# Routed rows written straight into their slots while the shared experts run, in place of one-hot lists and gathers

## Time and profile before

| what | us |
|---|---|
| median of 3 runs | 513.04 |
| lowest, highest | 508.51, 518.37 |
| the profiled execution, whole | 506.99 |
| the profiled execution, span | 505.3 |
| granted clock of TensorE, mean | 0.999 of full speed |

### The profile page before, as it was taken

One profiled execution on the slowest core, in us unless ns is written; L12 is line 12 of the kernel. 1 busy time (PEld: TensorE's weight loads), 2 busy tenths in 40 slices (PEclk: granted clock), 3 DMA queues, 4 the chain that ended last, 5 costly groups with the idle time before them and its releaser, 6 DMA issues.

```text
span 505.3 us, 10018 instructions
## 1 busy us (share of the span) xinstructions
PE 490.5 (97%) x3071; PEld 448.2 (89%) x3072; DVE 355.4 (70%) x765; ACT 261.1 (52%) x525; POOL 249.9 (49%) x367
## 2 busy tenths in 40 slices
PE   8999999999999999989999999999999899999996
PEld 7998988888888889988889999999998899888886
DVE  3666778898987556766676677676675666479896
ACT  3567785556663445565455555545554444444322
POOL 2042246655551454666967767677667674211100
PEclk9999999999999999999999999999999999999999
DMA  8387569156222234534344444444444442599942
GB/s 225 130 281 224 169 186 310 57 179 201 45 83 43 84 93 126 119 103 125 104 114 116 114 116 123 123 117 117 112 114 116 115 105 68 145 370 322 384 140 83
DMA packets 104938, 74.54 MB, mean 148 GB/s; under 512 B 61946, under 2 KB 99844, under 8 KB 104900
## 3 DMA queue, kind: packets, MB, share of 16 engines
q1 hardware_dynamic: 95780, 55.21, 37.1%
q0 software_dynamic: 6816, 18.62, 12.5%
q10 hardware_dynamic: 2304, 0.26, 0.5%
HBM read 40.25 MB, written 20.32 MB: 120 GB/s over the span
## 4 chain that ended last, share of the span: by engine, by line
PE 75%; DVE 15%; ACT 5%; issue 4%; DMA 1%; another core or an unknown queue 0%; DVEq 0%; ACTq 0%
PE bank L274 17%; PE bank L276 17%; PE bank L275 17%; PE bank L790 9%; PE bank L762 5%; PE bank L792 5%; DVE bank L1222 2%; ACT gt_h L952 1%; DVE acc L1333 1%; DVE xt_l L1034 1%; ACT x_half L872 1%; DVE x L1058 1%; DVE pos L1081 1%; DMA xin<-in_x_dram 1%; PE bank L576 1%
## 5 line engine op out<-in xcount | busy, mean ns | idle before, releaser
L274 PE MATMUL bank<-w_all,rt_h 128*128 x284 | 97.6, 344 | 0.0
L276 PE MATMUL bank<-w_all,rt_l 128*128 x284 | 91.6, 323 | 0.0
L275 PE MATMUL bank<-w_all,rt_h 128*128 x284 | 91.5, 322 | 0.0
L790 PE MATMUL bank<-w_all,gt_h 128*128 (+1 forms) x213 | 78.0, 396 | 0.2 <-issue 0.2
L551 POOL DMA_INDIRECT y_rows<-y_sb,dst_i x71 | 72.5, 1021 | 11.2 <-POOL spare L465 10.4
L544 POOL DMA_INDIRECT rows<-x_halves,tok_i x71 | 69.5, 978 | 12.5 <-issue 2.2
L952 ACT CAST gt_h<-bank 128x512 fp32r<-128x512 f32 (+1 forms) x48 | 28.1, 586 | 88.7 <-DVE bank L1222 79.8
L274 PE MATMUL bank<-xs_h,sg_h 128*128 128x512 f32 x176 | 70.6, 401 | 0.3 <-DVE gt_h L1233 0.3
L275 PE MATMUL bank<-xs_l,sg_h 128*128 128x512 f32 x176 | 68.9, 391 | 0.0
L276 PE MATMUL bank<-xs_h,sg_l 128*128 128x512 f32 x176 | 68.7, 390 | 0.0
L1295 DVE TENSOR_TENSOR g<-bank,act 128x352 f32<-128x352 f32 x71 | 37.2, 524 | 41.7 <-issue 24.5
(11 more groups left out here) (180 smaller groups left out, 1155.6 us busy)
## 6 DMA issues: line engine op xcount, KB each, us to landing
pick<-y_rows SPq DMA_DIRECT2D x16, 512.0 KB, 7.8
xin<-in_x_dram SPq DMA_DIRECT2D x8, 512.0 KB, 4.8
x_halves<-x_half SPq DMA_DIRECT2D x8, 512.0 KB, 3.3
w_own<-in_L_ffn_w_gate_dram SPq DMA_DIRECT2D x8, 352.0 KB, 4.5
w_own<-in_L_ffn_w_up_dram SPq DMA_DIRECT2D x8, 352.0 KB, 4.7
y_sb<-in_x_dram SPq DMA_DIRECT2D x5, 512.0 KB, 3.5
base_rows<-y_sb SPq DMA_DIRECT2D x5, 512.0 KB, 2.8
acc<-base_rows SPq DMA_DIRECT2D x5, 512.0 KB, 7.1
```

Source lines behind the costliest of these rows:

```text
L274: pe.matmul(o, lh, rh, start=start, stop=False, skip_group_check=skip)
L275: pe.matmul(o, lh, rl, start=False, stop=False, skip_group_check=skip)
L276: return pe.matmul(o, ll, rh, start=False, stop=stop, skip_group_check=skip)
L790: pe.matmul(YE[par][:, 0:2 * D].rearrange("p (h d) -> p h d", h=2), gt_h[par][0:n, cols], both, start=(c == 0), stop=False, skip_group_che ...
```

## The change

No list of rows by slot is made. While the shared experts run, SP loads each 128-row tile of `x1_halves` into SBUF, twice side by side (`load_stage`, 4 buffers), POOL puts the number of the output row behind each row (`number`), and two indirect DMAs of 128 rows write the tile to its slots in a new DRAM tensor `slot_rows` of 9088 rows of 1056 bytes (`put`, 64 of them, with 7 more for the empty slots). The routed stage then turns the rows of a block straight from `slot_rows` (`turn_rows`, four buffers), and reads all output row numbers back in one DMA (9088 elements of 4 bytes) into `dst_i`. POOL does no gathers.

Low halves of experts 2 to 7 and of groups 2 to 4 move from POOL to DVE (`weights_low`, `rows_low`). DVE's one-hots and `list_out`, and PE's 64 `permute` matmuls go. `rank` moves one unit on. The weights of the two choices (7 small DVE steps) move to unit 25. In the routed stage `r_high(1)`/`e_silu(0)` and `r_low(1)`/`e_mul(0)` change places. At the very end the last low half is made in two pieces, and one of the last three stores is issued by ACT. The core of the diff (buffers and semaphores left out):

```diff
@@ SP
+        STORE_AT = (6, 9, 18, 28)
+            def load_stage(t):
+                b = t % N_STAGE
+                sp.wait_ge(s_put[b], 16 * (pads_in(b) + TOPK * (t // N_STAGE)))
+                sp.dma_start(stage[b][:, :, 0:2 * D], x1_dram[t * P:(t + 1) * P, :].rearrange("(o p) d -> p o d", o=1)
+                             .broadcast_to([P, TOPK, 2 * D])).then_inc(s_stage[b], 16)
             def turn_rows(i):
-                sp.wait_ge(s_row[i % 3], 16 * (i // 3 + 1))
-                if i >= 2:
-                    sp.wait_ge(s_rlo, i - 1)
-                    sp.wait_ge(s_rhi, i - 1)
-                sp.dma_start_transpose(turned[i % 2][:], rows[i % 3][:]).then_inc(s_turn[i % 2], 16)
+                if i >= 4:
+                    sp.wait_ge(s_rlo, i - 3)
+                    sp.wait_ge(s_rhi, i - 3)
+                sp.dma_start_transpose(turned[i % 4][:], slot_dram[i * P:(i + 1) * P, 0:2 * D]).then_inc(s_turn[i % 4], 16)
...
             load_expert(5)
+            store_base(0)
+            load_res(1)
+            for t in range(4):
+                load_stage(t)
             sp.wait_ge(s_blk, 1)
             load_expert(7)
             load_expert(6)
-            for j in range(NPG - 1):
-                store_base(j)
-                load_res(j + 1)
-                if j + 3 <= NPG:
-                    load_raw(j + 3, raw)
+            for t in range(4, NT):
+                if t in STORE_AT:
+                    j = STORE_AT.index(t)
+                    if j >= 1:
+                        store_base(j)
+                        load_res(j + 1)
+                    if j + 3 <= NPG:
+                        load_raw(j + 3, raw)
+                load_stage(t)
+            for b in range(N_STAGE):
+                sp.wait_ge(s_put[b], 16 * (pads_in(b) + TOPK * (NT // N_STAGE)))
+            sp.wait_ge(s_top_w, 1)
             for i in range(4):
                 turn_rows(i)
+            sp.dma_start(dst_i[:].bitcast(U16).rearrange("p (b h) -> p b h", h=2),
+                         slot_dram[:, 2 * D:2 * D + 2].rearrange("(b p) h -> p b h", p=P)).then_inc(s_dst, 16)
+            for i in range(4, 6):
+                turn_rows(i)
             store_base(NPG - 1)
-            for i in range(4, NBLK):
+            for i in range(6, NBLK):
                 turn_rows(i)
@@ POOL
+            def number(b):
+                return stage[b][:, :, 2 * D:2 * D + 2].bitcast(I32)
+            def put(b, c, where):
+                pool.indirect_dma_start(slot_dram, bass.IndirectOffsetOnAxis(ap=where, axis=0),
+                                        stage[b][:, c, :], None).then_inc(s_put[b], 16)
             pool.wait_ge(s_x1, NT)
...
+            for i in range(2):
+                pool.wait_ge(s_x1st[i], 16 * (NG // 2))
+            for b in range(N_STAGE):
+                ins = pool.memset(stage[b][:], 0)
+            link(ins)
+            for n in range(PADS):
+                b, c = n % N_STAGE, n // N_STAGE
+                link(pool.tensor_copy(number(b)[:, c, :], pad_ids[:, n:n + 1]))
             split_low(1)
             pool.wait_ge(s_mark, 1)
...
             routed_low(1)
-            routed_low(2)
...
-            routed_low(6)
+            pool.wait_ge(s_pad_i, 1)
+            for n in range(PADS):
+                put(n % N_STAGE, n // N_STAGE, pad_i[:, n:n + 1])
+            pool.wait_ge(s_slot_i, 1)
+            for t in range(NT):
+                b = t % N_STAGE
+                pool.wait_ge(s_stage[b], 16 * (t // N_STAGE + 1))
+                link(pool.tensor_copy(number(b), ids[:, :, t:t + 1]))
+                for c in range(TOPK):
+                    put(b, c, slot_i[:, c, t:t + 1])
...
-            for i in range(5):
-                gather(i)
+            pool.wait_ge(s_dst, 16)
             for i in range(NBLK):
-                if i + 5 < NBLK:
-                    gather(i + 5)
                 if i == 14:
                     split_low(NPG)
                 scatter(i)
@@ PE
                 gate(j, c)
+                if u == RANK_AT + 1:
+                    rank()
                 if u >= 2:
                     down(*order[u - 2])
-                for t in hot_tiles(u - 2):
-                    permute(t)
                 up(j, c)
-                if u == RANK_AT:
-                    rank()
@@ DVE
+            def weights_low(e, i):
+                own_ap, hi, lo = routed_part(e, i)
+                v.wait_ge(s_whi, TURN_OF[e] * N_PART + i + 1)
+                v.tensor_tensor(lo, own_ap, hi.bitcast(F32), ALU.subtract).then_inc(s_wlo, 1)
...
-            steps_at = {0: (0, 8), 1: (3, 6), 2: (3, 6), 3: (3, 6), 4: (3, 1000), 5: (0, 6), 6: (0, 6), 7: (3, 7), 8: (3, 1000)}
+            steps_at = {0: (0, 8), 1: (3, 6), 2: (3, 6), 3: (1, 0)}
+            places_at = {4: (0, 4), 5: (3, 6), 6: (3, 6), 7: (3, 8), 8: (3, 1000)}
+            low_at = {10: (2, 0), 11: (2, 2), 13: (3, 0), 14: (3, 2), 16: (4, 0), 17: (4, 2), 19: (5, 0), 20: (5, 2),
+                      22: (7, 0), 23: (7, 2), 26: (6, 0), 27: (6, 2)}
...
+                if c in (2, 3) and j + 1 in BY_V:
+                    rows_low(j + 1, c - 2)
+                if u in low_at:
+                    e, i = low_at[u]
+                    weights_low(e, i)
+                    weights_low(e, i + 1)
+                if u == NPRE - 5:
+                    some(weigh, 1000)
```

228 lines of the change are left out of this document (96 added, 132 removed).

## The result

The changed kernel took 535.76 us (median of 4 runs, 535.27 to 539.57) beside 511.88 us (4 runs) for the kernel before on the same chip: ratio 1.053, 95% interval 1.044 to 1.061, slower. The forecast was 523.0 us, slower by 1.9%. Its direction and its place hold; the chain cost more than twice what was forecast. The profiled execution took 539.57 us, its span is 537.8 us.

A forecast was written before the change was run, and what follows sets the result against it. PE bounds the kernel, busy 490.5 of 505.3 us. Terms -4.2 + 13.3 + 2.0 + 0 - 0.5 - 0.6 = +10.0 us gave 523.0 us, 1.9% slower; the 8-in-10 range was 500 to 536 us.

The forecast's parts named there:

- +13.3: PE's stall in us before its first routed block, wanted at 181.3 us and ready at 194.6; bounds 7.1 and 20.2.
- (c): POOL's pitch per tile: number write 0.18, 0.17 until the put, two puts of 1.02, gaps 0.06: 2.45 us.
- (b): Seven pad puts on POOL, 1.02 us each and 0.02 between two; POOL begins tile 0 at about 103 us.
- (d): SP's queue delays tile 9's load behind ACT's split and `load_raw(4)`: POOL stands 6.1 us; other stops under 1 us.
- Rival 3: DVE's 30 low halves hold up POOL's number writes: +3.4 us in the chain, 526.4 us; chance 0.10.
- the first case: The chain of puts is late as forecast, PE waiting for `rt_l(0)`: range 512 to 531 us, chance 0.45.
- Removed on PE: Before the routed stage: permutes 3.0 us, wait for the count 0.6, DVE relief 0.6: -4.2 us; bounds 0 and -5.
- The 4-byte reads: The `dst_i` DMA of 9088 pieces delays the turn of block 4: 2 us of stall, ends 0 and 20.
- rival 4: The 4-byte reads are dear: 31 us on the rings, +20 instead of +2, 541 us; chance 0.08.
- 13 us of cover: In the routed stage, scatters waiting for `dst_i` have four buffers, some 13 us before they hold anybody.
- The routed stage: Gaps of 6.7 us ahead of transposes L762 not tied to gathers: 0 taken, ends 0 and -6.7.
- Rival 2: Chain in time and routed-stage gaps lost: -12.0 us, 501.0 us on the median; chance 0.15.

The follow-up runs named there:

- a_fill2: The kernel after with 130 transposes of the identity on PE ahead of its wait for the first `rt_l`: 536.57 us, ratio 1.072.
- a_no_puts: The kernel after without stage loads, pad puts, puts and the 4-byte DMA of `dst_i`; turns read x1 in its own order: 497.76 us.
- a_loads: The kernel after without puts but with the 32 stage loads kept, spaced over DVE's units; turns read x1 in its own order: ratio 0.971.
- the pair of one chip: The kernel after with 130 added transposes (a_fill2), 536.57 us, and with ACT copies replacing DVE's 24 low halves of weights, 536.69 us.
- a_again: The kernel after, unchanged, profiled beside the kernel before on one chip: ratio 1.059.
- a_dst_late: The kernel after, complete, with the 4-byte DMA of `dst_i` issued behind the last store of base rows: 532.83 us.
- the twins: The kernel after, 539.99 us, and the same kernel with the `dst_i` DMA behind the last store of base rows (a_dst_late), 532.83 us.
- b_no_gather: The kernel before without its 71 gathers on POOL; the transposes read x1 from DRAM in its own order: 502.42 us.
- a_dst_fill: The kernel after with late `dst_i` (a_dst_late) and 24 identity transposes on PE behind the last stage-3 put's landing: 532.61 us.

## Why the prediction was right or wrong

**Right:** the place (PE ahead of its first w_all matmul, released by `rt_l`), the sign, a stop at tile 9 behind SP's queue, and the saving in the shared stage. The step that failed is the price of the chain of puts, the term "+13.3", which measured 30.3 us. **Its root is (c)**, "0.06 us of gaps" in a tile, with (b)'s "0.02 between two" of the same source. The rows it came from the earlier trace rows have each indirect DMA behind a tiny write of POOL, which itself starts at once; between two indirect DMAs without one there are 0.30 us. From tile 0 to the last put the forecast had 187.6 - 103 = 84.6 us, and the trace 212.9 - 110.7 = 102.2:

```
                                          forecast   measured   difference
tile 0 taken up                              103       110.7       +7.7
pitch, 32 tiles                           32 x 2.45  32 x 2.69     +7.7
COPYs and puts longer than their best          0         5.7       +5.7
stops                                        6.1        10.0       +3.9
last put ends                              187.6       212.9      +25.3
to PE's first w_all matmul                   7.0         5.8       -1.2
```

(The 5.7 us are 64.7 - 64 x 0.96 and 8.5 - 32 x 0.19.) The four terms give 25.0; the last 0.3 us are gaps slightly longer than their best. Of the 25.3 us 7.0 don't reach the stall, since PE too was later than forecast (188.3 against 181.3 us). Tile 0 was late by 5.0 us of a slower start, by 1.4 us of `pad_i`, and by the gaps of 0.3 us between the pads with a longer first put. The stops: (d) took one, of 6.1 us, for ACT's split ahead of `load_raw(4)`. The split was there, and ended at 135.11 us, just before `load_raw(4)` went out; but of the same time the queue had stood 3.6 us for the landing of the store of base rows ahead of `load_res(2)`, which (d) had at nothing. In a_fill2 that wait alone held it (split ended at 129.64 us, `load_raw(4)` issued at 130.70), and in the kernel after it came again before tile 18, where (d) had less than 1 us and 3.8 came. The pitch's upper bound, 2.75, held the bare pitch, but no bound was kept for puts that DVE lengthens, and the mean of all tiles without stops is (102.2 - 10.0) / 32 = 2.88.

**Rival 3** was right in its mechanism and came on top of the first case, which the forecast priced as if they excluded each other. It said that "the rows show it for POOL's element-wise work only", and that indirect DMAs beside such instructions took 0.99 to 1.07 us and "show nothing like it". That was read from two rows. The trace of before has five indirect DMAs, all scatters, that began inside an L1264; four took 1.22 to 1.25 us, where 1.01 is the median, and the fifth is the 1.07 us of the earlier trace rows, with 0.19 us of the L1264 left. One of the four (POOL, then DVE):

```profile
393.60 1.25 POOL L551 DMA_INDIRECT y_rows<-y_sb,dst_i  x1 [0.16 <-POOL spare L465]
393.55 0.42 DVE L1264 TENSOR_TENSOR rt_l<-rt_w,rt_h 128x256 fp32r<-128x256 f32 x1
```

(The one L1264 of 1.68 us began inside POOL's two L504 and ended 0.29 us behind them.) Its 3.4 us were 3.6 in the pair of one chip, which is luck: it priced the writes of numbers alone, and these were 1.2, the puts 2.4. By the rule named in the prediction (the Trainium skill, SBUF — State Buffer, section "SBUF: two separate sides") a DVE instruction of two SBUF inputs contends only with work of POOL that reads SBUF. The runs agree if a put counts as such work: the eight puts above took 0.3 to 0.5 us longer. Which SBUF read of a put meets it is not shown.

**Removed on PE:** forecast -4.2; the shared stage fell by 4.5 us in a_no_puts and 3.7 in a_loads. In the kernel after 2.0 are left: the puts took the rest, and in a_again and a_dst_late, where the stage took 147 and 148 us, far more, under cover of the stall.

**The 4-byte reads:** the term was +2.0, on the ground that turn 4 would be late. It wasn't. The cost, 4.0 us of PE in the profile and 7.2 us between the twins, came by another way that the step had not followed: SP's queue behind them, with the last store of base rows, which frees `y_sb` for `e_y(0)`. The DMA itself landed 8.1 us after its issue, near the lower estimate of 9.9, so rival 4's 31 us on the rings, and its 20 of stall, fall. The "13 us of cover" held for the scatters; of what stands behind the pieces on the queue only the turns were followed.

**The routed stage:** "I take 0" was wrong, the end of -6.7 was right: 243.1 us against 234.7 (a_no_puts), 235.6 (b_no_gather), 235.7 (a_dst_fill). Rival 2 was right in this half, and a_no_puts, at 15.5 us below the kernel before, is that rival without its chain. In the kernel after the gain is hidden: -8.4, then +4.0 for `e_y(0)`, some 2 for the clock at half, and the rest, some 2, is not accounted for.

**Not foreseen:** the clock behind a long stall (1.9 us), and 5.0 us at the start, whose cause stays open.

In sum, against the forecast of +10.0: the stall 30.3 instead of 13.3, the 4-byte reads 4.0 instead of 2.0, the clock some 2, the shared stage -2.0 instead of -4.2, the start +5.0; against that the gaps of the routed stage, -8.4 instead of 0. That makes some 30 of the 32.6 us between the two profiles. Between the medians there are 23.9, and which terms are smaller in the other executions isn't shown. 535.76 us lies inside the stated 500 to 536 us, but outside the 512 to 531 of the case that came: the wide range held it, not the sum.
